# Running maxima of a graph-attention layer, made one turn ahead of the products that use them, with one-hots for two sets and the overflow tile merged through GpSimd

## The reference, cut to what matters

```
def segment_softmax(scores, seg, num_segments):
    smax = jax.ops.segment_max(scores, seg, num_segments=num_segments)
    sexp = jnp.exp(scores - smax[seg])
    ssum = jax.ops.segment_sum(sexp, seg, num_segments=num_segments)
    return sexp / ssum[seg]
...
att = jnp.sum(Qh * Kh, axis=-1)
alpha = segment_softmax(att, row, num_nodes)
```

## Time and profile before

| | us |
|---|---|
| median of 3 runs | 10467.82 (10465.63 to 10472.99) |
| the profiled execution | 10462.73 |
| its span, first to last instruction | 10461.2 |
| busy in it: PE, PEld | 8085.6, 6641.9 |
| busy in it: DVE, ACT, POOL | 8031.5, 4527.8, 1394.2 |
| mean granted clock of TensorE | 0.835 of full speed |
| the changed phase | about 3411 to 3998 |

### The profile page before, as it was taken

The page is one execution under the profiler, slowest core; times in us unless marked ns, Lnnn a source line. Parts: engine busy times, 40 slices in busy tenths (PEclk is TensorE's granted clock), DMA queues, the critical chain, the costliest instruction groups (busy, mean ns, idle before and its releaser), DMA issues. The chain is left out here.

```text
span 10461.2 us, 308127 instructions
## 1 busy us (share of the span) xinstructions
PE 8085.6 (77%) x93666; PEld 6641.9 (63%) x93814; DVE 8031.5 (77%) x16702; ACT 4527.8 (43%) x9123; POOL 1394.2 (13%) x1711
## 2 busy tenths in 40 slices
PE   2335666758888456999986998898999779579996
PEld 0232225547777446999984666346999746378886
DVE  4987777779999666666667998777888777788887
ACT  0220002236666114666654443786777556323333
POOL 0110001210000002666550000000000012100000
PEclk7555555559999557999998999999999989889998
DMA  2000004424444112333324887785555400000000
GB/s 55 0 7 8 5 5 141 147 77 163 161 162 155 38 37 81 123 123 121 124 95 162 271 273 245 259 292 159 144 144 144 115 5 6 3 4 3 3 3 14
DMA packets 613317, 1065.91 MB, mean 102 GB/s; under 512 B 120883, under 2 KB 266554, under 8 KB 606967
## 3 DMA queue, kind: packets, MB, share of 16 engines
q1 hardware_dynamic: 489222, 890.58, 26.8%
q10 hardware_dynamic: 113040, 161.93, 4.2%
q0 software_dynamic: 10976, 12.53, 0.4%
HBM read 868.94 MB, written 195.84 MB: 102 GB/s over the span
## 5 line engine op out<-in xcount | busy, mean ns | idle before, releaser
L2548 POOL TENSOR_TENSOR acc<-acc,m_sum 128x544 f32<-128x544 f32 (+1 forms) x637 | 811.0, 1273 | 1225.5 <-ACT m_sum L2515 1185.2
L2412 DVE TENSOR_TENSOR m_msg<-m_vps,m_msg 128x512 f32<-128x512 f32 (+1 forms) x637 | 427.7, 671 | 409.4 <-PE m_vps L2453 371.2
L2477 PE MATMUL m_sps<-m_msg,m_oh 128*128 128x136 f32 x4900 | 697.5, 286 | 0.0
L2884 PE MATMUL u_sps<-u_r,u_oh 128*128 128x129 f32 x4900 | 657.2, 275 | 28.7 <-ACT u_r L2840 28.7
L1545 ACT COPY sp_adj_x<-sp_aps_x 128x512 f32<-128x512 f32 (+1 forms) x637 | 363.0, 570 | 724.2 <-PE sp_aps_x L1516 724.2
L1532 PE MATMUL sp_out_x<-x,sp_adj_x 128*128 128x128 f32 x4802 | 672.8, 284 | 0.0
L1516 PE MATMUL sp_aps_x<-sp_ohw_x,sp_oh_x 128*128 128x128 bf16 x7350 | 537.3, 221 | 166.1 <-DVE sp_ohw_x L1483 166.0
L2117 PE MATMUL s_qps<-q_parts,s_oht 128*128 128x128 bf16 x7203 | 511.5, 220 | 198.6 <-DVE s_oht L1599 146.9
L2868 PE MATMUL u_zps<-fcs,u_a 128*128 128x128 f32 x4916 | 655.1, 276 | 7.2 <-ACT u_a L2833 7.2
L2884 PEld LDWEIGHTS u_sps<-u_r,u_oh 128*128 128x128 f32 x4900 | 599.0, 192 | 37.6 <-issue 37.6
L2477 PEld LDWEIGHTS m_sps<-m_msg,m_oh 128*128 128x128 f32 x4900 | 609.9, 190 | 0.0
(11 more groups left out here) (590 smaller groups left out, 19682.3 us busy)
## 6 DMA issues: line engine op xcount, KB each, us to landing
u_e<-e_tiles SPq DMA_DIRECT2D x591, 256.0 KB, 2.8
e_tiles<-t_es ACTq DMA_DIRECT2D x588, 256.0 KB, 4.2
g_e<-e_tiles SPq DMA_DIRECT2D x588, 256.0 KB, 4.5
s_rows<-bucket_rows SPq DMA_DIRECT2D x148, 768.0 KB, 4.1
m_rows<-bucket_rows SPq DMA_DIRECT2D x148, 768.0 KB, 4.1
bs_krow<-bucket_keys SPq DMA_DIRECT2D x49, 1600.0 KB, 7.0
t_rows<-bucket_rows SPq DMA_DIRECT2D x148, 384.0 KB, 5.2
s_rows<-bucket_rows SPq DMA_DIRECT2D x49, 896.0 KB, 5.1
```

Of the source, the lines that this page charges most:

```text
L2477: last = nc.tensor.matmul(sps[x][:, at:at + M], oh[x][:, j * P:(j + 1) * P], msg[x][:, j * M:(j + 1) * M], start=True, stop=True)
L2548: nc.gpsimd.tensor_tensor(at, at, sums[x][:, 0:n * M], ALU.add).then_inc(added, 1)
L2884: last = nc.tensor.matmul(sps[:, :], oh[x][:, j * P:(j + 1) * P], zr[x][:, j * D1:(j + 1) * D1], start=(q == 0 and j == 0), stop=(q == las ...
```

## The change

- **A turn ahead.** The scan of window w+1, its turning back, the three casts and the two subtractions now stand in turn w, beside the products of window w. The three part tiles `x_part0` to `x_part2` get twice their size, and turn w uses the half `(w & 1) * W`, written by ScalarE's casts and read by VectorE's subtractions and by the products. On TensorE the back-turn of w+1 and the turn of w+2 stand behind the second of seven groups of products. The first window's steps stand ahead of the loop.
- **One-hots for two sets.** `twos` pairs the sets: six pairs and one single. A one-hot is 1024 columns, there are three buffers and a spare one for the last (`Ring(len(twos), 3, True)`), and the first two groups of w+1 are made at the end of turn w, ahead of the large maximum.
- **The overflow tile.** Its product goes to a tile of its own (`eps`), which ScalarE copies to `extra`. GpSimd reads the block's number, copies the block's 8 columns of `most` to `held`; VectorE takes the larger of `held` and `extra` in the next turn (`larger`), and GpSimd copies that back into `most`. VectorE's large maximum waits for it (`merged`). VectorE reads no table any more.
- **Loads.** Scores are loaded when the window before has been turned; mask and ends are loaded apart, with a semaphore each.

The diff, cut to its core:

```diff
-    R = Ring(NQ, 4)
+    twos = [range(q, min(q + 2, NQ)) for q in range(0, NQ, 2)]
+    last = len(twos) - 1
+    R = Ring(len(twos), 3, True)
...
-        rest, parts = sb("x_rest", W), [sb(f"x_part{c}", W, BF16) for c in range(3)]
-        oh = [sb(f"x_oh{r}", GE, BF16) for r in range(R.size)]
+        rest, parts = sb("x_rest", W), [sb(f"x_part{c}", 2 * W, BF16) for c in range(3)]
+        oh = [sb(f"x_oh{r}", 2 * GE, BF16) for r in range(R.size)]
...
             @block.tensor
...
-                with pe.Fori(0, B.windows(pe, s)) as w:
-                    pe.wait_ge(scanned, w + 2)
+                def turn_back(w):
+                    pe.wait_ge(scanned, w + 3)
                     pe.wait_ge(split, w * 5 + 1)
...
-                    turn(w + 1)
+                turn(0)
+                turn_back(0)
+                turn(1)
+                with pe.Fori(0, nw) as w:
+                    half = (w & 1) * W
                     pe.wait_ge(split, w * 5 + 6)
-                    pe.wait_ge(maxed, w * (OV + 1) + 1)
-                    for q in range(NQ):
-                        r = R.slot(q)
-                        pe.wait_ge(oh_made[r], R.before(w, q) + 1)
-                        for j in range(B.held(q)):
-                            t = q * G + j
-                            for c in range(3):
-                                last = nc.tensor.matmul(mps[:, t * H:(t + 1) * H], of_pair(oh[r][:, :], P, j),
-                                                        parts[c][:, (j * NQ + q) * H:(j * NQ + q + 1) * H], start=(c == 0), stop=(c == 2))
-                        last.then_inc(used[r], 1)
+                    pe.wait_ge(maxed, w + 1)
+                    pe.wait_ge(extra_set, w + 1)
+                    for d, sets in enumerate(twos):
+                        r = R.slot(d)
+                        pe.wait_ge(oh_made[r], R.before(w, d) + 1)
+                        for q in sets:
+                            for j in range(B.held(q)):
+                                t = q * G + j
+                                into = mps[:, t * H:(t + 1) * H] if t < s.NB else eps[:, (t - s.NB) * H:(t - s.NB + 1) * H]
+                                for c in range(3):
+                                    end = nc.tensor.matmul(into, of_pair(oh[r][:, :], P, t - sets[0] * G),
+                                                           parts[c][:, bass.ds(half + (j * NQ + q) * H, H)], start=(c == 0), stop=(c == 2))
+                        end.then_inc(used[r], 1)
+                        if d == 1:
+                            turn_back(w + 1)
+                            turn(w + 2)
...
             @block.vector
...
+                with dve.Fori(0, nw) as w:
                     scan(w + 1)
-                    dve.wait_ge(split, w * 5 + 4)
-                    nc.vector.tensor_tensor(rest[:, :], rest[:, :], parts[1][:, :], ALU.subtract).then_inc(split, 1)
-                    for q in range(4, NQ):
-                        hot(q)
-                    dve.wait_ge(oh_made[r_last], R.before(w, NQ - 1) + 1)
+                    hot(w, 2)
+                    larger_of(w)
+                    hot(w, 3)
+                    lessen(w + 1, 0)
+                    hot(w, 4)
+                    lessen(w + 1, 1)
+                    for d in range(5, last + 1):
+                        hot(w, d)
+                    dve.wait_ge(oh_made[r_last], R.before(w, last) + 1)
                     dve.sem_inc(free, 1)
-                    dve.wait_ge(used[r_last], R.before(w, NQ - 1) + 2)
+                    hot(w + 1, 0)
+                    hot(w + 1, 1)
+                    dve.wait_ge(used[r_last], R.before(w, last) + 2)
+                    dve.wait_ge(merged, w + 1)
                     nc.vector.tensor_tensor(most[:, 0:S], most[:, 0:S], mps[:, 0:S], ALU.max).then_inc(maxed, 1)
-                    for j, v in enumerate(vs):
-                        dve.wait_ge(maxed, w * (OV + 1) + (j + 2))
-                        nc.vector.tensor_tensor(most[:, bass.ds(v * H, H)], most[:, bass.ds(v * H, H)], mps[:, S + j * H:S + (j + 1) * H],
-                                                ALU.max).then_inc(maxed, 1)
...
             @block.scalar
...
-                    nc.scalar.copy(parts[0][:, :], bps[:, :]).then_inc(split, 1)
+                    part = parts[c][:, (w & 1) * W:(w & 1) * W + W] if isinstance(w, int) else parts[c][:, bass.ds((w & 1) * W, W)]
+                    nc.scalar.copy(part, rest[:, :] if c else bps[:, :]).then_inc(split, 1)
...
+                    nc.scalar.copy(extra[:, :], eps[:, :]).then_inc(extra_set, 1)
+            @block.gpsimd
...
+                    for j, v in enumerate(vs):
+                        end = nc.gpsimd.tensor_copy(held[:, j * H:(j + 1) * H], most[:, bass.ds(v * H, H)])
+                    end.then_inc(held_set, 1)
+                    pool.wait_ge(larger_set, w + 2)
+                    pool.sem_inc(merge_go, 1)
+                    for j, v in enumerate(vs):
+                        end = nc.gpsimd.tensor_copy(most[:, bass.ds(v * H, H)], larger[:, j * H:(j + 1) * H])
+                    end.then_inc(merged, 1)
```

More of the change, by code:

```diff
@@ L2172, in _, with load_att @@
                 nw = B.windows(sp, s)
[L2174 to L2175 removed]
+                def load_att(n, w):
                     sp.wait_ge(turned, n + 1)
[L2177 removed]
                     sp.sem_inc(go, 1)
@@ L2199, in turn @@
                     pe.wait_ge(att_in, w * 32 + 32)
[L2200 removed]
+                    pe.wait_ge(scanned, w + 2)
                     for j in range(G):
[L2202 to L2206 removed]
+                        end = nc.tensor.transpose(tps[0:HQ, j * P:(j + 1) * P], att[:, j * HQ:(j + 1) * HQ], k["ident"][:, :])
@@ L2207, in _ @@
+                    end.then_inc(turned, 1)
+                def turn_back(w):
+                    pe.wait_ge(scanned, w + 3)
                     pe.wait_ge(split, w * 5 + 1)
                     for j in range(G):
-                        last = nc.tensor.transpose(bps[:, j * HQ:(j + 1) * HQ], run[:, j * P:(j + 1) * P], k["ident"][0:HQ, 0:HQ])
-                    last.then_inc(back, 1)
-                    turn(w + 1)
-                    pe.wait_ge(split, w * 5 + 6)
-                    pe.wait_ge(maxed, w * (OV + 1) + 1)
@@ new lines, in lessen, with hot @@
+                def lessen(w, c):
+                    dve.wait_ge(split, w * 5 + (2 + 2 * c))
+                    part = parts[c][:, (w & 1) * W:(w & 1) * W + W] if isinstance(w, int) else parts[c][:, bass.ds((w & 1) * W, W)]
+                    nc.vector.tensor_tensor(rest[:, :], rest[:, :] if c else bps[:, :], part, ALU.subtract).then_inc(split, 1)
+                def hot(w, d):
+                    r, n, at = R.slot(d), sum(B.held(q) for q in twos[d]), twos[d][0] * G
+                    if d == 0:
+                        dve.wait_ge(ends_in, w * 16 + 16)
+                    dve.wait_ge(used[r], R.before(w, d) + 1)
+                    values = ends[:, at:at + n] if isinstance(w, int) else ends[:, bass.ds((w & 1) * NT + at, n)]
+                    pair_hot(nc, oh[r][:, 0:n * P], k["iota1_2"], P, values, n // 2).then_inc(oh_made[r], 1)
@@ L2270, in _, with cast @@
+                dve.wait_ge(merged, nw + 1)
+                dve.sem_inc(zeroed, 1)
             @block.scalar
             def _(act):
-                r_last = R.slot(NQ - 1)
-                with act.Fori(0, B.windows(act, s)) as w:
-                    act.wait_ge(back, w + 2)
-                    act.wait_ge(used[r_last], R.done(w, r_last) + 1)
-                    nc.scalar.copy(parts[0][:, :], bps[:, :]).then_inc(split, 1)
-                    act.wait_ge(split, w * 5 + 3)
-                    nc.scalar.copy(parts[1][:, :], rest[:, :]).then_inc(split, 1)
-                    act.wait_ge(split, w * 5 + 5)
-                    nc.scalar.copy(parts[2][:, :], rest[:, :]).then_inc(split, 1)
+                def cast(w, c):
+                    if c:
+                        act.wait_ge(split, w * 5 + (1 + 2 * c))
+                    part = parts[c][:, (w & 1) * W:(w & 1) * W + W] if isinstance(w, int) else parts[c][:, bass.ds((w & 1) * W, W)]
+                    nc.scalar.copy(part, rest[:, :] if c else bps[:, :]).then_inc(split, 1)
@@ new lines, in _ @@
+                act.wait_ge(back, 2)
+                for c in range(3):
+                    cast(0, c)
+                with act.Fori(0, B.windows(act, s)) as w:
+                    act.wait_ge(back, w + 3)
+                    for c in range(3):
+                        cast(w + 1, c)
+                    act.wait_ge(used[r_last], R.before(w, last) + 2)
+                    act.wait_ge(larger_set, w + 1)
+                    nc.scalar.copy(extra[:, :], eps[:, :]).then_inc(extra_set, 1)
+            @block.gpsimd
```

74 lines of the change are left out of this document (49 added, 25 removed).

## The result

The changed kernel takes 10846.21 us (median of 4 runs, 10844.13 to 10847.26) where the kernel before takes 10466.72 us beside it (10462.27 to 10472.99): 1.036 of its time, 95% interval 1.035 to 1.038. It is 3.6% slower, 42 us above the forecast of 10804 and inside the range of 10720 to 10900. The profiled execution has a span of 10845.7 us (10461.2 before), at a mean granted clock of 0.822 (0.835).

A forecast was written before the change was run, and what follows sets the result against it. No engine was full; a chain of waits set the 11.83 us turn. With TensorE's queue setting 18.6 us, 48 periods add 325 us and the ends 11: 10799 on the profiled execution, 10804 us as median, range 10720 to 10900.

The forecast's parts named there:

- The mechanism and the sign: In the changed loop, register instructions for the products' addresses pace TensorE's queue, making the kernel 3.2% slower; slower had 0.95.
- The fused ones: Register instructions of three fused operations, ahead of the first of each three products: 50 a turn at 125 ns each.
- The single ones: Single-operation register instructions ahead of the other two of each three products: 100 a turn at 110 ns each.
- The transposes: Eight transposes behind the fourth set of products: counted as covered, 0.3 us a turn for waits; uncovered 2.05 us.
- Rival 3: TensorE's queue stops at the transposes' waits, leaving them uncovered: 20.4 us a turn, 10892 us; chance 0.10.
- The restart: TensorE from last weight load through VectorE's maximum, 0.78 us, then 0.3 us for three register instructions before the first load.
- The sum: TensorE's turn: 17.25 + 0.78 + 0.3 + 0.3 = 18.6 us, against 11.83 before.
- At the ends: Outside the 48 periods: first products 13.1 us longer, first set 3.6 us earlier, last merge about 1 us: +11.
- 17.25 us: TensorE's products of a turn, 50 x 125 + 100 x 110 ns, where they were 4.1 us.
- Rival 1: TensorE's queue makes addresses ahead of time, so VectorE sets the turn at 8.2 us: 10291 us, faster; chance 0.04.
- Costed at nothing: Wide one-hots' savings, GpSimd's copies, ScalarE's copy and loads: zero while the turn exceeds 8.2 us, otherwise under 1 us a turn.
- The rule beside it: Records of queue-executed instructions exclude decoding and semaphore push; by records alone TensorE's register work would be 5.5 us a turn.

## Why the prediction was right, and where it was off

- **The mechanism and the sign** were right. The products' addresses come from a register, the register instruction paces TensorE's queue, and TensorE sets the turn. Taking the register out turns 3.6% slower into 1.7% faster, and putting it into the kernel before makes that one 6.5% slower.
- **The fused ones** were taken at 125 ns from another loop at the earlier trace rows, and they are 124. (The divisions printed there give 126, 127, 153 and 30 ns where the prediction has 125, 125, 152 and 28. The rounded lengths of the rows allow both, and nothing hangs on it.)
- **The single ones** were taken at 110 ns, the record of 32 and 78 more, within 97 to 125. They are 113, by the starts of the register records. So the record's length and a constant is a fair rule in this kernel: 46 and 78, 32 and 81, and 74 and 79 at L1350. The 2.6 ns too few are some 12 us over 100 products and 48 turns.
- **The queue's pauses are the term that was missing.** The forecast had the register instructions follow each other without a break. About 15 times a turn, eight register instructions apart and at places that come back every second turn, one of them starts 30 ns late; two more are 46 ns late and one 93. That is 0.64 us a turn, 31 us over 48 turns, and the larger part of the miss. It is why the products' average is 120 ns where the records say 350 / 3 = 117. What the queue does in these pauses no run shows.
- **The transposes** were counted at 0.3 us as covered. By the weight loads the gap looks larger: from the last of the 48 loads (3812.00 + 5.62) to the first behind the transposes (3819.25) it is 1.63 us. But the queue goes on making addresses meanwhile, and the following loads catch up. By the register records it loses 0.47 us there, for four register and semaphore instructions that stand ahead of the transposes; its pace behind them is the same 124 and 113 ns while the eight transposes execute. That is 8 us of the miss. Rival 3 (uncovered, 20.4 us a turn) didn't occur.
- **The restart** was 0.78 + 0.3 = 1.08 us. Measured from the last load's start (3810.67 + 0.21) to the next turn's first (3812.00): 1.12.
- **The sum** of a turn by the register records: 50 x 124 + 99 x 113 ns = 17.4 us, pauses 0.64, the instructions ahead of the transposes 0.47, the restart 1.09. That is 19.6 us, against the 19.55 measured and the 18.6 predicted. 48 times the difference is 45 us. At the ends I had +11, and it is 14: the first maximum's 10.6 and what the spans leave behind the last (384.5 - 370.7 - 10.6).
- **Luck** made the miss smaller. On the profiled execution it is 10847 against 10799, 48 us. The prediction then added 5.1 us because the median had stood that far above the profiled execution; in the changed kernel it stands 1.1 us below, which gives 6 back. And the 17.25 us hold 150 products although the 0.78 us run from the last load's start, so that one product is counted twice; without it the forecast would have been 5 us lower.
- **Rival 1** had VectorE alone set the turn at 8.2 us, 10291 us in all. That is the kernel with static halves almost to the microsecond, 8.22 us and 10290.48. But the agreement is partly luck: VectorE is busy for 321.56 of 380 us there, 7.0 us a turn. Of the 8.2 us I had counted 7.7 as work, the one-hots among it at 4.6 us where they take 4.2, and 1.2 us of waits and issue fill the rest.

```profile
3440.00:3820.00 380.00, 279.49 (x7322) 257.43 (x7320) 321.56 (x557) 80.69 (x185) 91.64 (x93) 0.50 0.19 53
```

- **"Costed at nothing"** held for the loads and GpSimd's copies only while the turn was over 8.2 us, as the prediction said. In the fast kernels both matter: GpSimd's merge is worth 25 to 48 us, and the load queue nothing or some 25 to 34, depending on the order of the others.
- **The rule beside it**, of the Trainium skill, page "Perfetto Trace Analysis", section on the per-instruction lifecycle: that the record of an instruction which the sequencer executes itself is its execution alone. The traces agree. Records of 46 and 32 ns belong to register instructions after which the next starts 124 and 113 ns later.

## What to carry to other kernels

Double buffering with a register (`half = (w & 1) * W`) puts an address computation ahead of every instruction that reads the buffer. Where those are many and short, unroll the loop by two and give each copy a fixed half; it cost 120 ns against 27 for each product here, on the average. Look at what the queue has to do between two matmuls in the built program before you look at the array, and read the pace from the starts of the weight loads, since a queue that is starved of addresses reads as an engine that is 95% busy. When an order on one engine is improved and nothing is gained, look for the queue whose signal has been moved along with it.

## What the runs showed of the hardware that I had not expected

- Bare matmuls behind one with a register address are free: 124 ns for the three, as for the one alone. The eight transposes don't slow the queue's register work either.
- GpSimd's copy of 8 columns beside VectorE's scan lasts 0.19 us by its record in some kernels and seven times that in others, with the same instruction and the same data. The changed kernel, then the one with static halves (min/median/max ns):

```profile
L2343 POOL COPY x_held<-most x49: 189/190/191, 3440.5 to 4379.1; 128x8 f32 x49
```

```profile
L2349 POOL COPY x_held<-most x49: 190/1365/1370, 3432.5 to 3827.2; 128x8 f32 x49
```

It was 189 ns in the kernel with the late signal, 190 with narrow one-hots, and 1367 and 1475 in the two with moved load waits. In those with the long record, a one-hot of 1024 columns starts within 0.8 us of the copy's start, and the copy ends about when that one-hot does; in those with the short record the next wide one-hot starts later, or is narrow. Spans on GpSimd are rough, no experiment was made on it, and the cause stays open. It didn't keep the fastest kernel (1475 ns) from being the fastest.
